# Workspace FFN: an eighth of the output bias added by VectorE as it moves the projected values from PSUM, in place of a bf16 product and ScalarE's copies

## The chip, the cores and the metric

The kernel runs on one core of a Trainium2 chip. Five engines work side by side and meet at semaphores: TensorE (PE; its weight loads are PEld), VectorE (DVE), ScalarE (ACT), GpSimd (POOL) and SyncE (SP), which starts most transfers. The metric is the time of one execution on the device, in microseconds (us), as the median of several runs.

## The reference

The program is a small decoder over x of shape 64 x 128 x 512: an attention, a feed-forward layer with ternary weights, a causal attention, and last the part that matters here, a workspace layer, run twice over the same weights:

```python
for _ in range(NB):                                   # NB = 2
    logits = _rms(x, norm_pre_w) @ compete_w.T + compete_b
    vals, idx = top_k(swapaxes(logits, 1, 2), 4)      # 4 tokens for each of 16 slots
    wgt = softmax(vals)
    written = einsum('bsk,bskd->bsd', wgt, (x @ write_w.T + write_b)[idx])
    ws = _rms(ws + written, norm_post_w)
    q, kk, vv = x @ wq.T + bq, ws @ wk.T + bk, ws @ wv.T + bv    # 8 heads of 64
    att = softmax(einsum('blhd,bshd->bhls', q, kk) * scale)      # over 16 slots
    x_b = einsum('bhls,bshd->blhd', att, vv) @ out_proj_w.T + out_proj_b
    x = _rms(x + x_b, norm_post_w)
```

The kernel uses that the slots are few: it projects the values with out_proj_w first, for each head and slot, which gives 8 x 16 = 128 rows of 512 for a batch (VO), and multiplies the 128 x 128 attention weights of a batch with them. For each token the weights of one head sum to 1, so those of its 8 heads sum to 8.

## The kernel before

The last stage, `workspace_ffn`, works on eight batches at a time, a unit. There are 16 units: 8 groups of eight batches, each passed through twice (`first` and `second` pass). Two neighbouring groups alternate, and the function `step(f, u, after)` of each engine interleaves the front half of unit f (transposes of X, logits, top four slots, new slots ws, keys and values) with the back half of unit f - 1, called u (scores, softmax, values, output). `units` runs 17 such steps: two written out, three turns of a loop of four, three written out. Steps 1 to 15 have both halves, step 16 only the back one. In half of them u is the second pass; its results are added to the first input by GpSimd (`add_first`) and stored.

No scheduler decides: each engine executes its own step in the order in which it is written, and waits at semaphores. The back half has, for each batch b of its eight:

- `value_out(b)` on TensorE, four products into the one bank `vo_ps`; it waits until the bank has been moved for the batch before (`vo_done`);
- `values(b)`, the move of `vo_ps` to `VO[b % 2]` (line 1918, on ScalarE before the change);
- `mix(b)` on TensorE into `xb_ps[b % 2]`: a product of 96 rows of ones with `out_b_parts` (line 1772), then the attention weights with VO (line 1773). `out_b_parts` holds the bias as the sum of three bf16 numbers, in rows 0, 32 and 64;
- `residual(b)` on VectorE, y = xb_ps + X (line 1619), its squares' sum on ScalarE (line 1925), 1/rms on GpSimd (lines 1493, 1495), and `final(b)` on VectorE (line 1630).

A f32 product of 512 columns is two instructions in the trace. From the front half of the same step the argument touches the chain of the top slots on VectorE, `lg` (line 1664) to `is_top` (1673), `w_raw` (1675) and `w_top` (1679), which TensorE turns at line 1839; the new slots `ws` (1718), turned at line 1879 and copied as `wsT` for the key and value products (1780); and `turn_att` (1764) with its copy `d_attT` (1930) on ScalarE, for which the first mix of a step waits. A tile's name has the prefix `d_` in the trace.

Of the kernel before, what the change touches and what calls it, by code (L numbers as in the profile page):

```python
# [12 lines left out]
BF16 = mybir.dt.bfloat16  # L13
# [896 lines left out]
class WorkspaceState:  # L910
# [3 lines left out]
    def __init__(self, nc, st, x, ident, workspace, compete_wT, compete_b, write_wT, write_b, wq, wkT, wvT, in_proj_cols,  # L914
# [14 lines left out]
        self.out_b_parts, self.ones_rows = sb("out_b_parts", [96, C], BF16), sb("ones_rows", [96, 128], BF16)  # L929
# [13 lines left out]
        self.out_b_row, self.out_b_part = self.y[:, 0, :], self.junk2[0:96, :]  # L943
# [11 lines left out]
        for dst, src in ((self.write_b_row[:, :], write_b), (self.out_b_row, out_b), (self.post_row[:, :], norm_post)):  # L955
            self.small.append((dst, src.rearrange("(o n) -> o n", o=1).to_broadcast([128, C])))
# [3 lines left out]
                        (self.WT[:, :, :], 0.0), (self.out_b_parts[:, :], 0.0), (self.ones_rows[:, :], 1.0),  # L960
# [3 lines left out]
def causal_attention(nc, x, ctx, ctxT, ident, after, causal_cols, x_out, w):  # L964
# [12 lines left out]
    with ExitStack() as st:  # L977
# [143 lines left out]
        def _(dve):  # L1121
# [7 lines left out]
            def step(t):  # L1129
# [45 lines left out]
                if t.k == 57:  # L1175
                    dve.wait_ge(w.small_in, 16 * 23)
                    dve.wait_ge(w.preset, 9)
# [3 lines left out]
                if t.k == 58:  # L1181
                    dve.tensor_copy(w.out_b_part, w.out_b_row[0:96, :]).then_inc(w.const_ready, 1)
                    dve.wait_ge(w.const_ready, 4)
                    dve.tensor_copy(w.out_b_parts[0:1, :], w.out_b_part[0:1, :]).then_inc(w.const_ready, 1)
                    dve.tensor_tensor(w.out_b_row[0:96, :], w.out_b_row[0:96, :], w.out_b_part, ALU.subtract).then_inc(w.const_ready, 1)
                if t.k == 59:
                    dve.wait_ge(w.const_ready, 6)
                    dve.tensor_copy(w.out_b_part, w.out_b_row[0:96, :]).then_inc(w.const_ready, 1)
                    dve.wait_ge(w.const_ready, 7)
                    dve.tensor_copy(w.out_b_parts[32:33, :], w.out_b_part[32:33, :]).then_inc(w.const_ready, 1)  # L1190
                    dve.tensor_tensor(w.out_b_row[0:96, :], w.out_b_row[0:96, :], w.out_b_part, ALU.subtract).then_inc(w.const_ready, 1)
                    dve.wait_ge(w.const_ready, 9)
                    dve.tensor_copy(w.out_b_parts[64:65, :], w.out_b_row[64:65, :]).then_inc(w.const_ready, 1)
# [151 lines left out]
def workspace_ffn(nc, x, w, x_out):  # L1345
# [13 lines left out]
    with ExitStack() as st:  # L1359
# [10 lines left out]
        write_b_row, post_row, out_b_parts, ones_rows, neg_half = w.write_b_row, w.post_row, w.out_b_parts, w.ones_rows, w.neg_half  # L1370
# [11 lines left out]
        is_top, e_top, w_raw, w_top = sb("is_top", [128, 128]), sb("e_top", [128, 128]), sb("w_raw", [128, 128]), sb("w_top", [128, 128])  # L1382
# [187 lines left out]
        def _(dve):  # L1570
# [16 lines left out]
            def step(f, u, after):  # L1587
# [25 lines left out]

                def residual(b):
# [45 lines left out]
                if f.exists():  # L1660
# [12 lines left out]
                    link(5, dve.tensor_tensor(is_top[:, :], lg_out[:, 0:128], lg[:, 0:128], ALU.not_equal))  # L1673
                    dve.wait_ge(e_top_done, n + 1)
                    dve.scalar_tensor_tensor(w_raw[:, :], e_top[:, :], 1.0, is_top[:, :], ALU.mult, ALU.mult, accum_out=w_sum[:, :]).then_inc(top_chain, 1)
# [3 lines left out]
                    dve.tensor_scalar(w_top[:, :], w_raw[:, :], w_inv[:, :], None, ALU.mult).then_inc(w_top_done, 1)  # L1679
# [17 lines left out]
                if u.exists():  # L1697
                    final(2)
# [10 lines left out]
                if u.exists():  # L1709
# [372 lines left out]
```

## Time and profile before

| | |
|---|---|
| median of 3 runs | 3844.27 us (3840.09 to 3847.71) |
| profiled execution, its time | 3834.83 us |
| its span in the trace | 3832.5 us |
| busy in the span: TensorE, its weight loads | 3597.9 us (94%), 1956.2 us (51%) |
| VectorE, ScalarE, GpSimd | 2818.8 us (74%), 2526.4 us (66%), 1747.7 us (46%) |
| `workspace_ffn`, from about 2930 us on | 902.5 us |

Times in rows are us from the start of the span unless marked ns. A row of a timeline gives start, length, engine, line of the kernel, operation, output <- inputs, shapes and a count; in brackets stands how long the engine had been idle before it, and which instruction ended that. Ends of matmuls are modelled, and the next one may start before the end shown. The profiled execution is one run, 9.4 us below the median of the others.

### The profile page before, as it was taken

What the parts mean: (1) busy time and instruction counts of PE and PEld (TensorE: products, weight loads), DVE (VectorE), ACT (ScalarE), POOL (GpSimd) and SP (SyncE); (2) the same over time, 40 slices, a digit from 0 to 9 for tenths busy, and PEclk for the clock granted to TensorE, in tenths of its full rate; (3) what the DMA queues carried; (4) which work ended last, traced back from release to release, by engine and by line L of the source; (5) the groups of instructions that cost most, each with busy time, mean ns of one, the idle gap of its engine ahead of it and who ended that gap; (6) DMA issues with size and microseconds to landing.
All of it is one profiled execution on the core that took longest, in us unless ns stands there. A gap on an engine that the chain in (4) does not pass through costs nothing. (4 is left out here: it accounts for less than half of the span.)

```text
span 3832.5 us, 87056 instructions
## 1 busy us (share of the span) xinstructions
PE 3597.9 (94%) x24963; PEld 1956.2 (51%) x24963; DVE 2818.8 (74%) x4439; ACT 2526.4 (66%) x6353; POOL 1747.7 (46%) x2154
## 2 busy tenths in 40 slices
PE   5999999999999999699999979999998999999997
PEld 1222222222222222277777857777776666556664
DVE  5888888888888889577777757777775555464645
ACT  2777777777777777577767757777774554545454
POOL 6444444444444443266666625454553233342524
PEclk9999999999999999899999999999998999999999
DMA  7777777777777777333333323333452022120302
GB/s 117 122 123 122 121 121 121 124 121 122 125 124 123 121 121 147 107 111 109 112 103 112 106 67 102 101 107 99 140 160 75 1 68 67 47 87 8 127 1 78
DMA packets 344164, 389.94 MB, mean 102 GB/s; under 512 B 58640, under 2 KB 223120, under 8 KB 343952
## 3 DMA queue, kind: packets, MB, share of 16 engines
q1 hardware_dynamic: 317328, 352.82, 42.3%
q10 hardware_dynamic: 26624, 34.63, 3.5%
q8 instruction: 93, 1.52, 0.2%
q14 instruction: 119, 0.97, 0.1%
HBM read 200.65 MB, written 84.93 MB: 75 GB/s over the span
## 5 line engine op out<-in xcount | busy, mean ns | idle before, releaser
L372 DVE TENSOR_REDUCE a_neg_max<-a_max_ps 128x2 f32<-128x1024 f32 x1024 | 1200.2, 1219 | 188.6 <-PE a_max_ps L461 165.3
L493 ACT ACTIVATE a_P<-a_ring_ps 128x512 f32<-128x512 f32 x2048 | 1084.5, 604 | 384.4 <-PE a_ring_ps L443 379.8
L461 PE MATMUL a_max_ps<-a_K,a_Q 96*128 96x512 bf16 x2048 | 621.2, 385 | 44.7 <-DMA a_K<-a_k_split 39.5
L443 PE MATMUL a_ring_ps<-a_Q,a_K 98*128 98x512 bf16 x2048 | 618.1, 382 | 5.5 <-DMA a_Q<-a_max_rows 3.3
L478 PE MATMUL a_pv_ps<-a_P,a_V 128*32 128x512 f32 x4096 | 544.9, 604 | 1.8 <-ACT a_out_sb L498 1.8
L443 PEld LDWEIGHTS a_ring_ps<-a_Q,a_K 98*128 98x128 bf16 x2048 | 158.1, 96 | 658.7 <-ACT a_P L493 585.2
L1295 ACT ACTIVATE c_P<-c_s_ps,c_bias 128x128 f32<-128x128 f32 x1024 | 363.3, 377 | 50.9 <-DVE c_bias L1140 44.1
L319 POOL TENSOR_SCALAR a_var_eps<-a_mean_var 128x1 f32<-128x1 f32 x64 | 12.2, 190 | 648.6 <-DVE a_mean_var L388 648.3
L461 PEld LDWEIGHTS a_max_ps<-a_K,a_Q 96*128 96x128 bf16 x2048 | 182.6, 98 | 224.3 <-DVE a_neg_max L372 46.6
L1135 DVE TENSOR_REDUCE c_neg_max<-c_s_ps 128x4 f32<-128x512 f32 x256 | 176.7, 690 | 128.8 <-PE c_s_ps L1230 128.0
L1266 PE MATMUL c_bank_b<-c_V,c_PT 128*128 128x32 f32 x2048 | 251.6, 267 | 2.9 <-DVE c_PT L1158 2.9
L1266 PEld LDWEIGHTS c_bank_b<-c_V,c_PT 128*128 128x128 f32 x2048 | 249.7, 192 | 5.3 <-DVE c_PT L1158 4.1
L1295 ACT ACTIVATION_READ_ACCUMULATOR c_P<-c_s_ps,c_bias 128x1 f32 x1024 | 221.4, 216 | 0.0
L478 PEld LDWEIGHTS a_pv_ps<-a_P,a_V 128*32 128x32 f32 x4096 | 81.1, 108 | 218.1 <-issue 214.2
L1228 PE MATMUL c_s_ps<-c_KD,c_qT 64*128 64x256 f32 x1024 | 181.7, 432 | 2.9 <-ACT c_P L1295 2.1
L1619 DVE TENSOR_TENSOR d_y<-d_xb_ps,d_X 128x512 f32<-128x512 f32 x128 | 88.2, 690 | 94.3 <-PE d_xb_ps L1773 91.4
L843 PE MATMUL b_t_ps<-w_had,b_u 128*128 128x256 f32 x512 | 155.9, 386 | 1.5 <-DVE b_u L763 1.5
L1240 PE MATMUL c_pT_ps<-c_identf,c_P 128*128 128x128 f32 x1024 | 156.8, 276 | 0.0
L844 PE MATMUL b_t_ps<-w_had,b_u 128*128 128x256 f32 x512 | 152.3, 379 | 0.0
L674 POOL TENSOR_TENSOR b_scaled<-b_o_in,b_r_in 128x512 f32<-128x512 f32 x64 | 82.7, 1292 | 150.6 <-DMA b_r_in<-recips 98.4
L1925 ACT ACTIVATE d_junk<-d_y 128x512 bf16<-128x512 f32 x128 | 80.3, 627 | 94.1 <-DVE d_y L1619 93.2
L1098 POOL TENSOR_SCALAR c_z<-c_x_in,c_mean_var,c_rstd 128x512 f32<-128x512 f32 x64 | 133.2, 2081 | 16.8 <-POOL c_rstd L1095 15.0
(259 smaller groups left out, 7100.5 us busy)
## 6 DMA issues: line engine op xcount, KB each, us to landing
a_Q<-a_q_split SPq DMA_DIRECT2D x384, 128.0 KB, 4.6
a_K<-a_k_split SPq DMA_DIRECT2D x384, 128.0 KB, 7.4
heads_out<-a_out_sb ACTq DMA_DIRECT2D x128, 256.0 KB, 4.1
a_x_in<-in_x_dram SPq DMA_DIRECT2D x64, 256.0 KB, 3.7
a_c_in<-in_ctx_dram SPq DMA_DIRECT2D x64, 256.0 KB, 4.1
a_cT_in<-in_ctxT_dram SPq DMA_DIRECT2D x64, 256.0 KB, 4.1
b_x_in<-in_x_dram SPq DMA_DIRECT2D x64, 256.0 KB, 2.8
b_o_in<-heads_out SPq DMA_DIRECT2D x64, 256.0 KB
```

The costliest lines, as they stand in the source:

```text
L372: dve.tensor_reduce(neg_max[:, p, 2 * u:2 * u + 2], max_ps[u % 2][:, :, :], AX.X, ALU.max, negate=True).then_inc(max_taken, 1)
L443: pe.matmul(ring(s, use_of(k))[:, :], K[i][:, h, n:n + 128], Q[i][:, h, :], start=True, stop=True).then_inc(scores_filled, 1)
L461: last = pe.matmul(max_ps[u % 2][:, j, :], Q[i][0:KROW, h, m:m + 128], K[i][0:KROW, h, :], start=True, stop=True)
L478: last = pe.matmul(pv_ps[32 * j:32 * j + 32, :], V[i][:, t, p * G + j, :], P[p][j][:, t, :], start=(t == 0), stop=(t == NT - 1))
L493: act.activation(P[p][k // NT][:, k % NT, :], ring(s, use_of(k))[:, :], ACT.Exp, scale=SCALE).then_inc(exp_done, 1)
L843: pe.matmul(t2_ps[:, k * 128:(k + 2) * 128], u[i][:, k, :], had[:, 0:256], start=True, stop=False)
L844: last = pe.matmul(t2_ps[:, k * 128:(k + 2) * 128], u[i][:, k + 1, :], had[:, 128:384], start=False, stop=True)
L1135: dve.tensor_reduce(neg_max[:, i, c * G:(c + 1) * G].rearrange("p (r g) -> p r g", r=2), s_ps[:, c % 2, :, 0:256].rearrange("p r (g k) -> ...
L1228: pe.matmul(s_ps[:, c % 2, r, 0:256], qT[i][rows, c, :], KD[i][rows, c], start=True, stop=False)
L1240: last = pe.transpose(pT_ps[c % 2][:, g, :], P[:, i, c * G + g, :], identf[:, :])
L1266: last = pe.matmul(bank_b[:, h * D:(h + 1) * D], PT[i][:, h, :], V[t.slot(back, 4)][:, h * D:(h + 1) * D], start=True, stop=True)
L1295: act.activation(P[:, i, h, :], s_ps[:, c % 2, g // 2, g % 2 * 128:g % 2 * 128 + 128], ACT.Exp, scale=SCALE, bias=bias[:, i, h:h + 1], acc ...
```

## The change

The bias no longer goes through TensorE. An eighth of it is added to each row of VO; since the weights of a token sum to 8 over the heads and slots, the product of mix(b) contains the whole bias. The add is made by VectorE in the move from PSUM, which ScalarE's copy did before. The eight moves of a step are placed by hand into VectorE's program. Seven operations of the stage before, which split the bias into three bf16 rows, make way for one that divides it by 8:

```diff
-        self.out_b_parts, self.ones_rows = sb("out_b_parts", [96, C], BF16), sb("ones_rows", [96, 128], BF16)
+        self.out_b_row = sb("out_b_row", [128, C])
...
                 if t.k == 58:
-                    dve.tensor_copy(w.out_b_part, w.out_b_row[0:96, :]).then_inc(w.const_ready, 1)
...
-                    dve.tensor_copy(w.out_b_parts[64:65, :], w.out_b_row[64:65, :]).then_inc(w.const_ready, 1)
+                    dve.tensor_scalar(w.out_b_row[:, :], w.out_b_row[:, :], 1.0 / 8, None, ALU.mult).then_inc(w.const_ready, 1)
...
+                def values(b):
+                    m = u.n() * NB + b
+                    dve.wait_ge(vo_filled, m + 1)
+                    at_least(dve, xb_filled, m - 1)
+                    dve.tensor_tensor(VO[b % 2][:, :], vo_ps[:, :], out_b_row[:, :], ALU.add).then_inc(vo_done, 1)
...
                     softmax_sum(0)
                     softmax_sum(1)
+                if u.exists():
+                    values(0)
+                    values(1)
...
                     link(5, dve.tensor_tensor(is_top[:, :], lg_out[:, 0:128], lg[:, 0:128], ALU.not_equal))
+                if u.exists():
+                    values(2)
+                if f.exists():
                     dve.wait_ge(e_top_done, n + 1)
...
                     residual(1)
+                    values(3)
...
                     residual(2)
+                    values(4)
                     final(1)
...
+                    values(5)
                     final(2)
...
+                    values(6)
                     final(4)
                     residual(5)
+                    values(7)
...
-                    pe.matmul(xb_ps[b % 2][:, :], ones_rows[:, :], out_b_parts[:, :], start=True, stop=False)
-                    pe.matmul(xb_ps[b % 2][:, :], attT[b // 4][:, b % 4, :], VO[b % 2][:, :], start=False, stop=True).then_inc(xb_filled, 1)
+                    pe.matmul(xb_ps[b % 2][:, :], attT[b // 4][:, b % 4, :], VO[b % 2][:, :], start=True, stop=True).then_inc(xb_filled, 1)
...
-                    act.activation(VO[b % 2][:, :], vo_ps[:, :], ACT.Copy).then_inc(vo_done, 1)
```

Two tiles are saved besides: w_raw is written over e_top and w_top over is_top. The line numbers after the change differ.

On VectorE, in the loop's fourth body (a step whose u is a first pass), between the mask of the top slots and the copy of the turned weights, the rows of before are these (REGISTER_ALU and ISA rows set a wait's count or a semaphore):

```order
L1673 TENSOR_TENSOR d_is_top<-d_lg_out,d_lg 128x128
L1590 REGISTER_ALU
L1675 SCALAR_TENSOR_TENSOR d_w_raw,d_w_sum<-d_e_top,d_is_top 128x128
L1676 REGISTER_ALU
L1677 RECIPROCAL d_w_inv<-d_w_sum 128x1
L1678 ISA
L1679 TENSOR_SCALAR d_w_top<-d_w_raw,d_w_inv 128x128
L1617 REGISTER_ALU
L1619 TENSOR_TENSOR d_y<-d_xb_ps,d_X 128x512
L1684 COPY d_WT<-d_F 128x8x16
L1630 SCALAR_TENSOR_TENSOR d_X<-d_y,d_y_r,d_post_row 128x512
```

and after the change these:

```order
L1672 TENSOR_TENSOR d_is_top<-d_lg_out,d_lg 128x128
L1579 REGISTER_ALU
L1606 REGISTER_ALU
L1608 TENSOR_TENSOR d_VO<-d_vo_ps,d_out_b_row 128x512
L1677 SCALAR_TENSOR_TENSOR d_e_top,d_w_sum<-d_e_top,d_is_top 128x128
L1678 REGISTER_ALU
L1679 RECIPROCAL d_w_inv<-d_w_sum 128x1
L1680 ISA
L1681 TENSOR_SCALAR d_is_top<-d_e_top,d_w_inv 128x128
L1615 TENSOR_TENSOR d_y<-d_xb_ps,d_X 128x512
L1606 REGISTER_ALU
L1608 TENSOR_TENSOR d_VO<-d_vo_ps,d_out_b_row 128x512
```

The move of batch 2 has come between is_top and the weights' chain (w_raw is now d_e_top, w_top is d_is_top), and that of batch 3 behind the residual of batch 1.

Also on VectorE, in the same body, from ws_sum to ws, before:

```order
L1708 TENSOR_TENSOR d_ws_sum<-d_F,d_ws_first 128x512
L1630 SCALAR_TENSOR_TENSOR d_X<-d_y,d_y_r,d_post_row 128x512
L1617 REGISTER_ALU
L1619 TENSOR_TENSOR d_y<-d_xb_ps,d_X 128x512
L1718 SCALAR_TENSOR_TENSOR d_ws<-d_ws_sum,d_ws_r,d_post_row 128x512
```

and after:

```order
L1713 TENSOR_TENSOR d_ws_sum<-d_F,d_ws_first 128x512
L1606 REGISTER_ALU
L1608 TENSOR_TENSOR d_VO<-d_vo_ps,d_out_b_row 128x512
L1626 SCALAR_TENSOR_TENSOR d_X<-d_y,d_y_r,d_post_row 128x512
L1615 TENSOR_TENSOR d_y<-d_xb_ps,d_X 128x512
L1606 REGISTER_ALU
L1608 TENSOR_TENSOR d_VO<-d_vo_ps,d_out_b_row 128x512
L1725 SCALAR_TENSOR_TENSOR d_ws<-d_ws_sum,d_ws_r,d_post_row 128x512
```

The moves of batches 6 and 7 now stand ahead of ws, the first before final(4), the second behind residual(5).

On TensorE, in the same body, from the transpose of lr to mix(2), before:

```order
L1829 MATMUL d_F<-d_identf,d_lr 128x128
L1764 MATMUL d_SC<-d_identf,d_att 128x128 x4
L1756 MATMUL d_vo_ps<-d_wo_sb,d_vd 32x512 x4
L1772 MATMUL d_xb_ps<-d_out_b_parts,d_ones_rows 128x512
L1773 MATMUL d_xb_ps<-d_VO,d_attT 128x512
L1756 MATMUL d_vo_ps<-d_wo_sb,d_vd 32x512 x4
L1772 MATMUL d_xb_ps<-d_out_b_parts,d_ones_rows 128x512
L1773 MATMUL d_xb_ps<-d_VO,d_attT 128x512
```

and after:

```order
L1835 MATMUL d_F<-d_identf,d_lr 128x128
L1771 MATMUL d_SC<-d_identf,d_att 128x128 x4
L1763 MATMUL d_vo_ps<-d_wo_sb,d_vd 32x512 x4
L1779 MATMUL d_xb_ps<-d_VO,d_attT 128x512
L1763 MATMUL d_vo_ps<-d_wo_sb,d_vd 32x512 x4
L1779 MATMUL d_xb_ps<-d_VO,d_attT 128x512
```

Only the bias product of each mix is gone; the order of all else is kept.

## Rows read from the trace of the kernel before

**Rows 1.** Table of stretches, the last: busy us of each engine (instructions), PEclk, DMA.
```profile
2930.00:3832.50 902.50, 822.49 (x6547) 535.50 (x6545) 470.27 (x911) 436.41 (x977) 317.23 (x460) 0.98 0.17 53
```

**Rows 2.** What TensorE waited for, 2930 to 3832.5: us, times, longest us.
```profile
PE d_F L1879 <- DVE d_ws L1718: 11.6, 7, 3.4
```

**Rows 3.** All instances of a line: minimum, median, maximum ns; first and last start.
```profile
L1772 PE MATMUL d_xb_ps<-d_out_b_parts,d_ones_rows x128: 376/389/587, 2999.0 to 3818.6; 96*128 96x512 bf16 x128
...
L1918 ACT ACTIVATE d_VO<-d_vo_ps x128: 575/597/662, 2994.8 to 3815.9; 128x512 f32<-128x512 f32 x128
...
L1619 DVE TENSOR_TENSOR d_y<-d_xb_ps,d_X x128: 675/692/693, 3000.2 to 3822.1; 128x512 f32<-128x512 f32 x128
...
L1630 DVE SCALAR_TENSOR_TENSOR d_out_sb<-d_y,d_y_r,d_post_row x64: 741/752/1860, 3110.0 to 3825.3; 128x512 f32<-128x512 f32 x64
```

**Rows 4.** Timeline of TensorE in one step: start us, us, what, count, idle before.
```profile
3426.99 1.04 PE L1756 MATMUL d_vo_ps<-d_wo_sb,d_vd 128*32 128x512 f32 x8
...
3429.70 0.39 PE L1772 MATMUL d_xb_ps<-d_out_b_parts,d_ones_rows 96*128 96x512 bf16 x1 [0.87 <-ACT d_attT L1930]
...
3429.93 1.02 PE L1773 MATMUL d_xb_ps<-d_VO,d_attT 128*128 128x512 f32 x2
...
3432.65 1.02 PE L1773 MATMUL d_xb_ps<-d_VO,d_attT 128*128 128x512 f32 x2
...
3433.60 1.07 PE L1756 MATMUL d_vo_ps<-d_wo_sb,d_vd 128*32 128x512 f32 x8
...
3435.69 0.27 PE L1839 MATMUL d_F<-d_identf,d_w_top 128*128 128x128 f32 x1
...
3448.45 1.07 PE L1756 MATMUL d_vo_ps<-d_wo_sb,d_vd 128*32 128x512 f32 x8
...
3450.53 0.60 PE L1879 MATMUL d_F<-d_identf,d_ws 128*128 128x128 f32 x4
...
3452.05 3.73 PE L1780 MATMUL d_F<-d_wsT,d_wk_sb 128*128 128x128 f32 x32
```

**Rows 5.** Timeline of VectorE in the same step.
```profile
3426.45 0.35 DVE L1612 RECIPROCAL d_sc_inv<-d_sc_sum 128x32 f32<-128x32 f32 x1
...
3431.08 0.69 DVE L1619 TENSOR_TENSOR d_y<-d_xb_ps,d_X 128x512 f32<-128x512 f32 x1 [2.28 <-PE d_xb_ps L1773]
...
3431.69 0.34 DVE L1664 TENSOR_SCALAR d_lg<-d_F,d_cb_col 128x128 f32<-128x128 f32 x1
...
3433.65 0.29 DVE L1673 TENSOR_TENSOR d_is_top<-d_lg_out,d_lg 128x128 f32<-128x128 f32 x1
...
3433.97 0.29 DVE L1675 SCALAR_TENSOR_TENSOR d_w_raw<-d_e_top,d_is_top 128x128 f32<-128x128 f32 x1
...
3434.71 0.68 DVE L1619 TENSOR_TENSOR d_y<-d_xb_ps,d_X 128x512 f32<-128x512 f32 x1
...
3449.16 0.74 DVE L1718 SCALAR_TENSOR_TENSOR d_ws<-d_ws_sum,d_ws_r,d_post_row 128x512 f32<-128x512 f32 x1
```

**Rows 6.** Timeline of ScalarE in the same step: V(2) of before.
```profile
3432.91 0.59 ACT L1918 ACTIVATE d_VO<-d_vo_ps 128x512 f32<-128x512 f32 x1
```

**Rows 7.** Timelines of VectorE and TensorE one step earlier, at ws.
```profile
3396.86 0.75 DVE L1718 SCALAR_TENSOR_TENSOR d_ws<-d_ws_sum,d_ws_r,d_post_row 128x512 f32<-128x512 f32 x1 [1.78 <-POOL d_ws_r L1495]
...
3397.76 0.63 PE L1879 MATMUL d_F<-d_identf,d_ws 128*128 128x128 f32 x4 [1.35 <-DVE d_ws L1718]
```

**Rows 8.** Timelines of TensorE and VectorE in the last step.
```profile
3795.87 1.06 PE L1756 MATMUL d_vo_ps<-d_wo_sb,d_vd 128*32 128x512 f32 x8 [2.38 <-ACT d_VO L1918]
...
3796.23 0.35 DVE L1612 RECIPROCAL d_sc_inv<-d_sc_sum 128x32 f32<-128x32 f32 x1
```

**Rows 9.** TensorE's timeline at a turn of the loop and one step without it; PEclk there.
```profile
3249.96 9.04 PE L1791 MATMUL d_SC<-d_A,d_XT 128*128 128x128 f32 x64 [2.68 <-issue]
...
3412.76 7.41 PE L1791 MATMUL d_SC<-d_A,d_XT 128*128 128x128 f32 x64
...
3252.00:3254.00 2.00, 2.00 (x12) 2.00 (x10) 0.00 (x0) 1.91 (x7) 0.00 (x0) 0.50 0.00 0
```

More of the change, by code:

```diff
@@ L954, in __init__ @@
             self.small.append((self.ws_in[i * S:(i + 1) * S, :], workspace))
-        for dst, src in ((self.write_b_row[:, :], write_b), (self.out_b_row, out_b), (self.post_row[:, :], norm_post)):
+        for dst, src in ((self.write_b_row[:, :], write_b), (self.out_b_row[:, :], out_b), (self.post_row[:, :], norm_post)):
             self.small.append((dst, src.rearrange("(o n) -> o n", o=1).to_broadcast([128, C])))
@@ L1381, in workspace_ffn @@
         top, neg_top = sb("top", [128, 8]), sb("neg_top", [128, 1])
-        is_top, e_top, w_raw, w_top = sb("is_top", [128, 128]), sb("e_top", [128, 128]), sb("w_raw", [128, 128]), sb("w_top", [128, 128])
+        is_top, e_top = sb("is_top", [128, 128]), sb("e_top", [128, 128])
         w_sum, w_inv = sb("w_sum", [128, 1]), sb("w_inv", [128, 1])
@@ L1673, in step @@
                     link(5, dve.tensor_tensor(is_top[:, :], lg_out[:, 0:128], lg[:, 0:128], ALU.not_equal))
+                if u.exists():
+                    values(2)
+                if f.exists():
                     dve.wait_ge(e_top_done, n + 1)
-                    dve.scalar_tensor_tensor(w_raw[:, :], e_top[:, :], 1.0, is_top[:, :], ALU.mult, ALU.mult, accum_out=w_sum[:, :]).then_inc(top_chain, 1)
+                    dve.scalar_tensor_tensor(e_top[:, :], e_top[:, :], 1.0, is_top[:, :], ALU.mult, ALU.mult, accum_out=w_sum[:, :]).then_inc(top_chain, 1)
                     dve.wait_ge(top_chain, n * LINKS + 6)
@@ L1678, in step @@
                     dve.wait_ge(w_top_done, n * 2 + 1)
-                    dve.tensor_scalar(w_top[:, :], w_raw[:, :], w_inv[:, :], None, ALU.mult).then_inc(w_top_done, 1)
+                    dve.tensor_scalar(is_top[:, :], e_top[:, :], w_inv[:, :], None, ALU.mult).then_inc(w_top_done, 1)
                 if u.exists():
                     residual(1)
+                    values(3)
                 if f.exists():
@@ L1746, in _ @@
         def _(pe):
-            pe.wait_ge(const_ready, 10)
+            pe.wait_ge(const_ready, 4)
             def step(f, u, after):
@@ L1838, in step @@
                     pe.wait_ge(w_top_done, n * 2 + 2)
-                    pe.transpose(ft[:, 0:128], w_top[:, :], identf[:, :]).then_inc(wT_filled, 1)
+                    pe.transpose(ft[:, 0:128], is_top[:, :], identf[:, :]).then_inc(wT_filled, 1)
                 if u.exists():
@@ L1913, in step @@
             def step(f, u, after):
-                def values(b):
-                    m = u.n() * NB + b
-                    act.wait_ge(vo_filled, m + 1)
-                    at_least(act, xb_filled, m - 1)
-                    act.activation(VO[b % 2][:, :], vo_ps[:, :], ACT.Copy).then_inc(vo_done, 1)
                 def squares(b):
@@ L1956, in step @@
                         act.activation(sc_exp[:, half, :], sc[:, half, :], ACT.Exp, scale=SCALE).then_inc(sc_exp_done, 1)
-                if u.exists():
-                    values(0)
                 if f.exists():
@@ L1963, in step @@
                 if u.exists():
-                    values(1)
                     copy_att(0)
@@ L1967, in step @@
                     copy_att(1)
-                    values(2)
                 if f.exists():
@@ L1973, in step @@
                 if u.exists():
-                    values(3)
                     squares(1)
-                    values(4)
                 if f.exists():
@@ L1984, in step @@
                     squares(3)
-                    values(5)
                     squares(4)
@@ L1994, in step @@
                 if u.exists():
-                    values(6)
-                    values(7)
                     squares(5)
```

17 lines of the change are left out of this document (3 added, 14 removed).

## The prediction

> **What bounds the kernel now.** I read the table of stretches first, then what TensorE waits for in the last stretch, then one step there engine by engine. The last stretch, from 2930 on, is the workspace FFN, the only part whose work changes. There TensorE is busy 822 of 902.5 us, VectorE 470, ScalarE 436 [rows 1]. So TensorE sets the pace, and neither of the two engines between which work moves is full. That is an average, though. TensorE's own waits there are few and name their places: 11.6 us in seven steps before the transposes of the new slots [rows 2], and in a step 0.87 us before the first bias product, for ScalarE's copy of the turned weights [rows 4]. A step is a chain on TensorE with short detours over ScalarE or VectorE, and the question is whether a detour gets longer.
>
> I take the step that starts near 3412. Names: vo(b) is value_out(b), V(b) the move of its PSUM bank to SBUF (values), mix(b) the attention product, R(b) residual, F(b) final. vo(b+1) needs V(b), because there is one bank vo_ps.
>
> **What goes.** 128 bf16 products [rows 3]. A row's length, 0.39 us, is not what one costs: the f32 product behind it starts 0.23 us later (3429.70, 3429.93 [rows 4]). Eight a step are 1.8 us, over 16 steps 29 us: the most that can be won. ScalarE loses 128 copies of 0.60 us, VectorE gains 128 adds. The nearest row for such an add is R, one operand in PSUM, one in SBUF, the same shape: 0.69 us, between 0.675 and 0.693 in 128 cases [rows 3]; the next operation on VectorE starts 0.61 us after it (3431.08, 3431.69 [rows 5]). So each move takes 0.09 us more for those who wait, and VectorE's sum, 128 x 0.61 = 78 us, fits its idle time of 432 us. The few constant operations that go ran in the stage before, on a VectorE with idle time, beside TensorE's work: I cost them at nothing (two to three operations of 0.4 to 0.9 us in a step, should that cover be missing).
>
> **What the order makes of it.** VectorE executes in program order, so V(b) starts only when what stands ahead of it is done.
>
> *V(0)* stands behind both softmax sums. The last reciprocal starts at 3426.45 and takes 0.35; with the 0.32 us by which one short operation follows another (3433.65, 3433.97), V(0) runs 3426.77 to 3427.46. A consumer on TensorE starts 0.10 us after a copy ends (3432.91 + 0.59, then vo(3) at 3433.60 [rows 4, 6]), so vo(1) starts at 3427.56 instead of 3426.99: +0.57. The turned weights and their copy follow vo(1), and mix(0) waited already for that copy (0.87 us), so the delay goes through. Its bias product is gone, but the f32 product must now show its own weight load, which hid behind it: I take 0.10 us for that (bounds 0 and 0.2, a bias product's start being all that the row shows). Product of mix(0): +0.57 - 0.23 + 0.10 = **+0.44**. mix(1) leaves out another 0.23: +0.21.
>
> *V(2)* is the large one. It stands behind is_top, at the end of the chain of the top four slots. That chain begins with lg behind R(0), which waits for mix(0): lg 3431.69 + 0.44 = 3432.13. is_top follows 1.96 us later (3431.69, 3433.65), V(2) 0.32 behind it, at 3434.41, done at 3435.10; vo(3) at 3435.20 instead of 3433.60: **+1.60**. Before, ScalarE did this copy at 3432.91, beside the chain. vo(3) followed the product of mix(1) by 0.95 us, so TensorE is ready for it at 3432.86 + 0.95 = 3433.81, and a stall of about 1.4 us opens. Queued behind V(2) are w_raw to w_top and R(1). w_raw starts 0.61 behind V(2), at 3435.02, and R(1) 0.74 behind w_raw (3433.97, 3434.71), at 3435.76, w_top being done by about then. The transpose of w_top, L1839, is itself 1.37 us late, at 3437.06, so it waits for nobody.
>
> *mix(2) to mix(6)* leave out 5 x 0.23 = 1.15 us. Their moves V(3) to V(5) come in time: V(3) runs 3436.37 to 3437.06, and vo(4) stands behind L1839; the longer products L1848 and L1868 cover the next. vo(7) needs V(6), which starts when vo(6) ends and is done about 0.05 us later than TensorE is free for it. At mix(6) the step is +0.45.
>
> *V(7)* now stands ahead of ws (L1718). vo(7) is late by 1.60 - 4 x 0.23 = 0.68, starts at 3449.13 and ends 1.07 us later; V(7) starts some 0.06 behind that (an estimate: R starts 0.13 us behind the end of its product, 3429.93 + 1.02, then 3431.08), 3450.26, ws 0.61 later, 3450.87, and ends at 3451.61 (before it started at 3449.16 [rows 5]). With 0.15 us to TensorE (3396.86 + 0.75, then 3397.76 [rows 7]) the transposes L1879 start at 3451.76 instead of 3450.53: **+1.23**, a stall of 1.23 - 0.45 = 0.78 us that this step did not have. mix(7) gives 0.23 back, and L1780, 1.52 us behind L1879 before, needs the copy wsT, which ended just in time; that takes about 0.13 more. End of the step: **+1.13 us**. The half whose F goes to X has eight such steps: 9.0 us.
>
> The other half, whose output gets the first input added on GpSimd, waited for ws anyway: VectorE 1.78 us for GpSimd's d_ws_r, TensorE 1.35 us for ws [rows 7]. Removed bias products win nothing there, nor does V(7) cost: GpSimd's chain decides. It starts from R(2)'s squares, behind the copies of g on ScalarE, behind the products behind vo(4). So it comes as late as vo(4): +1.60 - 0.23 = +1.37. Seven such steps: 9.6 us.
>
> The last step, without a next unit, has vo(1) at 3795.87 for V(0), which ScalarE ended just before; VectorE's reciprocal runs until 3796.58 [rows 8], so V(0) ends near 3797.2: +1.4 us. Its later adds may or may not fit between the F's (0 to 6 x 0.61 = 3.7 us more); I take 0, as its bias products go too.
>
> **Sum.** 9.0 + 9.6 + 1.4 = 20.0 us slower, of which the removed products have been subtracted. The profiled execution took 3834.83 us, which lies 9.4 under the median of the runs, 3844.27; so a profiled one would take 3854.8, and the median **3864 us**. The likeliest case alone has a range of 3854 to 3875: weight loads shown fully or not (0.1 us x 15), a V to TensorE at 0.15 in place of 0.10 (three times a step, 2.3 us), the last step's 3.7, steps in which the top chain runs at another pace.
>
> **Rivals.**
> A, *the bias products are won.* Then the moves would be hidden and 29 us go: 3815. For it speaks VectorE's idle half of the stretch. Against it, its idle time isn't at V(0), V(2) and V(7). It decides if V(2) ends before 3433.7, 1.4 us earlier than I have it. Chance 0.09.
> B, *only V(2) stalls.* If the stall at V(0) and that at ws were hidden, each step would lose 0.44 + 0.78 less, 15 x 1.2 = 18 us: 3846, no change. The wait of 0.87 us for the turned weights would have to be slack and not a chain. Chance 0.10.
> C, *the clock falls.* At the loop's turn TensorE stood 2.68 us and then ran 64 products in 9.04 us where they take 7.41, its granted clock 0.50 of full, that is 1.2 GHz, for two of these [rows 9]. Three stalls in ten microseconds (0.6, 0.9 and 1.4 us) may do the same: 15 x 1.6 = 24 us more, 3888. Against it: in the other half stalls of 0.9 and 1.35 us passed without. [...] Chance 0.12.
> D, *F behind V meets GpSimd.* In the half with the first input added, F takes 1.86 us in place of 0.75 when it runs into a GpSimd add [rows 3]. Now that V(5) and V(6) stand before it, F(2) or F(4) may start inside such an add: one in each of seven steps, 7.7 us, 3872. The Trainium skill ("SBUF — State Buffer", two separate sides) has the pair of ports that both use locked by whoever starts first, and V, with one SBUF operand, outside of it; R's even 0.69 us agrees. Chance 0.05.
> My forecast has 0.64.
>
> **Numbers.** Slower in my case, C and D, and a little of B: 0.82. A change of 0.2%, 7.7 us, is about what a measurement of this kernel can tell from none; within it: 0.09, most of B. Faster: 0.09, A. The range leaves out A and the upper part of C: 3848 to 3884.
>
> **What would show it.** The profile after should have: no bf16 product, vo(3) waiting for d_VO by 1.3 to 1.6 us in 15 steps, with is_top to d_VO 0.32 us on VectorE; ws transposes waiting in all steps of both halves; V at 0.69 us; ScalarE's busy time down 76 us, VectorE's up 88; no half clock inside a step. Wrong would be the forecast if vo(3) waits for nothing, or if the time of TensorE between vo(0) and L1780 shrinks.

## The result, and the profile after

The changed kernel takes 3848.9 us (median of 20 runs, 3844.6 to 3857.9), the kernel before beside it 3838.2 (20 runs, 3832.3 to 3847.7): 1.0028 times as long, 95% interval 1.0021 to 1.0034, or 10.7 us slower. The forecast was 20.0 us slower, from 3844.3 to 3864. The three runs shown before the change lay 6.1 us above what 20 runs give; that shifts the forecast's time, not its difference. The profiled execution of after took 3844.60 us, its span is 3842.5, 10.0 above that of before.

The workspace stage of after, first its table of stretches (busy us and instructions of PE, PEld, DVE, ACT, POOL; PEclk, DMA), then what TensorE waited for:

```profile
2930.00:3842.50 912.50, 808.70 (x6400) 515.62 (x6400) 545.71 (x1032) 366.61 (x848) 317.46 (x458) 0.98 0.16 52
```

```profile
PE d_vo_ps L1763 <- DVE d_VO L1608: 25.8, 29, 3.7
PE d_F L1885 <- DVE d_ws L1725: 17.6, 16, 3.4
PE d_xb_ps L1779 <- ACT d_attT L1930: 11.5, 13, 1.0
...
PE d_F L1809 <- PEq L54: 6.9, 1, 6.9
```

VectorE's busy time is up 75.4 us, ScalarE's down 69.8, TensorE's down 13.8 [rows 1], and TensorE has a wait that it hadn't, for VectorE's V (25.8 us), and waits for ws in 16 steps where it was 7 [rows 2]. The same step as in [rows 4, 5], TensorE and then VectorE; it starts 0.54 us later than in before (scores at 3413.30, before 3412.76):

```profile
3427.93 1.06 PE L1763 MATMUL d_vo_ps<-d_wo_sb,d_vd 128*32 128x512 f32 x8 [0.23 <-DVE d_VO L1608]
...
3430.67 1.12 PE L1779 MATMUL d_xb_ps<-d_VO,d_attT 128*128 128x512 f32 x2 [0.87 <-ACT d_attT L1930]
3431.63 0.27 PE L1835 MATMUL d_F<-d_identf,d_lr 128*128 128x128 f32 x1
...
3435.63 1.06 PE L1763 MATMUL d_vo_ps<-d_wo_sb,d_vd 128*32 128x512 f32 x8 [1.25 <-DVE d_VO L1608]
3436.63 1.12 PE L1779 MATMUL d_xb_ps<-d_VO,d_attT 128*128 128x512 f32 x2
3437.59 0.27 PE L1845 MATMUL d_F<-d_identf,d_is_top 128*128 128x128 f32 x1
3437.80 1.06 PE L1763 MATMUL d_vo_ps<-d_wo_sb,d_vd 128*32 128x512 f32 x8
...
3449.97 1.07 PE L1763 MATMUL d_vo_ps<-d_wo_sb,d_vd 128*32 128x512 f32 x8
...
3452.60 0.63 PE L1885 MATMUL d_F<-d_identf,d_ws 128*128 128x128 f32 x4 [0.51 <-DVE d_ws L1725]
...
3453.93 3.83 PE L1786 MATMUL d_F<-d_wsT,d_wk_sb 128*128 128x128 f32 x32
```

```profile
3431.83 0.69 DVE L1615 TENSOR_TENSOR d_y<-d_xb_ps,d_X 128x512 f32<-128x512 f32 x1 [1.87 <-PE d_xb_ps L1779]
3432.44 0.34 DVE L1663 TENSOR_SCALAR d_lg<-d_F,d_cb_col 128x128 f32<-128x128 f32 x1
...
3434.40 0.29 DVE L1672 TENSOR_TENSOR d_is_top<-d_lg_out,d_lg 128x128 f32<-128x128 f32 x1
3434.89 0.69 DVE L1608 TENSOR_TENSOR d_VO<-d_vo_ps,d_out_b_row 128x512 f32<-128x512 f32 x1 [0.20 <-DVE d_is_top L1672]
```

That is the forecast's picture: vo(3) waits 1.25 us for V(2), which stands behind is_top. It does so in twelve of the 15 steps; in the other three (the first and the last two) the wait is 0.62 us. A length on the axis of the whole execution tells the rest. The columns below are worked out from each profile: **set-up**, from VectorE's first constant operation (d_cw, in causal attention) to TensorE's first X transposes of the workspace stage; **steps**, from the first score product of the first step that has them to that of the last, 15 steps; **end**, from there to the end of the span.

```
kernel                set-up   15 steps   end
before                102.0     803.1     47.4
after                  97.0     823.0     46.8
```

So the steps lost 20.0 us, and 5.0 us came back before they began, in a place that the prediction had costed at nothing. (Another 2.9 us of this pair of profiles lie ahead of the constants, in stages with the same code, 1.4 between the X transposes and the first step's score products, 0.7 at the end. The last two go with TensorE's clock: before is at half clock for 14.8 us between these transposes and the score products, after for 9.6; in the end before has a piece of 6.8 us at 3797 where after has one of 3.4.)

### The profile page after: what moved, and what is told of

Read it like the earlier page. It is cut to its first block and busy times, and to the rows that moved or that the text cites. A ratio compares the mean times of both kernels' runs of the same rounds, so it can differ in the third digit from the quotient of the medians.

```text
span 3842.5 us, 86727 instructions
## 1 busy us (share of the span) xinstructions
PE 3586.1 (93%) x24773; PEld 1941.2 (51%) x24835; DVE 2891.0 (75%) x4561; ACT 2458.4 (64%) x6225; POOL 1750.3 (46%) x2152
## 5 line engine op out<-in xcount | busy, mean ns | idle before, releaser
L1763 PE MATMUL d_vo_ps<-d_wo_sb,d_vd 128*32 128x512 f32 x1024 | 137.2, 608 | 26.2 <-DVE d_VO L1608 25.8
L1779 PE MATMUL d_xb_ps<-d_VO,d_attT 128*128 128x512 f32 x256 | 142.4, 638 | 14.8 <-ACT d_attT L1930 11.5
```

## The experiments

Each kernel was run 6 to 20 times beside before on the same chip; differences in us below are its ratio to that before, times 3838. An interval of 0.0010 is 3.8 us. All columns:

```
kernel                median us  ratio (95% interval)     diff   set-up  15 steps  end
after                 3848.9     1.0028 (1.0021, 1.0034)  +10.7   97.0    823.0    46.8
no_setup              3829.6     0.9975 (0.9966, 0.9985)   -9.6   97.0    805.1    44.7
no_product            3823.1     0.9953 (0.9938, 0.9968)  -18.0   97.0    795.0    44.4
vector_and_product    3855.1     1.0036 (1.0022, 1.0051)  +13.8   97.0    829.2    48.3
v2_early              3852.7     1.0032 (1.0020, 1.0043)  +12.3   97.0    823.8    49.5
scalar_234            3836.1     0.9990 (0.9981, 0.9999)   -3.8   97.0    806.6    50.1
scalar_67             3846.7     1.0019 (1.0010, 1.0028)   +7.3   97.0    817.8    49.2
setup_moved           3831.4     0.9978 (0.9969, 0.9986)   -8.4   97.0    803.4    47.4
setup_spread          3838.6     0.9986 (0.9977, 0.9995)   -5.4   99.2    803.3    47.5
before_again          3839.9     0.9997 (0.9986, 1.0007)   -1.2  102.2    805.1    44.5
before_third          3836.9     1.0001 (0.9991, 1.0010)   +0.4  101.9    803.3    47.4
pool_bias             3831.9     0.9982 (0.9973, 0.9991)   -6.9   97.0    806.5    47.1
pool_bias2            3850.7     1.0020 (1.0011, 1.0030)   +7.7   97.0    822.7    44.4
pool_bias3            3823.9     0.9968 (0.9958, 0.9978)  -12.3   97.0    797.0    45.7
```

**no_setup: before without the set-up.**

```diff
-                if t.k == 58:
-                    dve.tensor_copy(w.out_b_part, w.out_b_row[0:96, :]).then_inc(w.const_ready, 1)
...
-                    dve.tensor_copy(w.out_b_parts[64:65, :], w.out_b_row[64:65, :]).then_inc(w.const_ready, 1)
...
-            pe.wait_ge(const_ready, 10)
+            pe.wait_ge(const_ready, 3)
```

> The kernel before without the seven VectorE operations that split the output bias into three bf16 parts (the parts stay zero, so the bias is left out of the output; the bf16 product and ScalarE's copies stay). Between the first constant operation and the first X transposes of the workspace stage the profile of after is 5.0 us shorter than that of before: two seven-operation pieces hold VectorE in causal attention, TensorE then waits 1.17 us at 2863.85, and the granted clock is 0.50 to 0.65 from 2864 to 2872, which it is not after the change. Theory S (the set-up costs what that stretch shows): 4 to 6 us less than before, about 3833, and no stretch at half clock near there. Rival N (the earlier stages only differed from one execution to the next): within 1.5 us of before, 3838, the dip in the clock elsewhere or still there.

9.6 us less: Theory S, with more than it asked for. (The seven operations stand in two pieces, of three and of four.) Before shows how few microseconds of set-up cost 5. VectorE at the second piece, then TensorE behind it, then PEclk (the column behind the POOL pair):

```profile
2858.72 0.39 DVE L1188 CAST d_junk<-d_y 96x512 bf16<-96x512 f32 x1
2859.14 0.28 DVE L1190 COPY d_out_b_parts<-d_junk 1x512 bf16<-1x512 bf16 x1
2859.46 0.69 DVE L1191 TENSOR_TENSOR d_y<-d_y,d_junk 96x512 f32<-96x512 f32 x1
2860.18 0.88 DVE L1193 CAST d_out_b_parts<-d_y 1x512 bf16<-1x512 f32 x1
2861.09 0.69 DVE L1135 TENSOR_REDUCE c_neg_max<-c_s_ps 128x4 f32<-128x512 f32 x1
```

```profile
2862.08 0.60 PE L1240 MATMUL c_pT_ps<-c_identf,c_P 128*128 128x128 f32 x4
2863.85 1.08 PE L1266 MATMUL c_bank_b<-c_V,c_PT 128*128 128x32 f32 x8 [1.17 <-DVE c_PT L1158]
...
2869.59 1.23 PE L1228 MATMUL c_s_ps<-c_KD,c_qT 64*128 64x256 f32 x4
...
2872.91 0.70 PE L1228 MATMUL c_s_ps<-c_KD,c_qT 64*128 64x256 f32 x4
```

```profile
2864.00:2868.00 4.00, 4.00 (x24) 3.31 (x24) 3.77 (x6) 1.65 (x9) 1.59 (x2) 0.65 0.44 170
2868.00:2872.00 4.00, 4.00 (x18) 2.96 (x18) 0.61 (x1) 1.99 (x9) 0.00 (x0) 0.50 0.00 0
2872.00:2876.00 4.00, 4.00 (x29) 2.87 (x28) 3.76 (x13) 2.70 (x13) 2.42 (x3) 1.00 0.57 162
```

Four operations in a row hold the next c_PT back, TensorE waits 1.17 us, and then runs at 1.2 GHz (PEclk 0.50) for 6.8 us (0.35 and 0.50 of full missing in 4 us each) until 2872: the same four products take 1.23 us at 2869.59 and 0.70 at 2872.91. The whole stretch, before and then no_setup:

```profile
2837.00:2939.00 102.00, 92.18 (x673) 70.73 (x673) 82.55 (x168) 63.10 (x296) 48.76 (x47) 0.94 0.38 122
```

```profile
2836.45:2933.44 96.99, 88.65 (x673) 68.28 (x672) 77.04 (x161) 63.17 (x295) 48.18 (x47) 0.97 0.41 129
```

The same 673 products keep TensorE busy 3.5 us longer in before: that is the half clock. Its waits for c_PT are 1.5 us longer (2.9 for 1.4). Together 5.0. VectorE itself is idle 20 of the 97 us of no_setup, so its idle time is real, but not where the piece stands: in the same round it is idle for 0.37 and 0.40 us there, against a piece of 2.3 (no_setup):

```profile
2857.88 0.69 DVE L1135 TENSOR_REDUCE c_neg_max<-c_s_ps 128x4 f32<-128x512 f32 x1 [0.37 <-PE c_s_ps L1217]
...
2860.98 0.69 DVE L1135 TENSOR_REDUCE c_neg_max<-c_s_ps 128x4 f32<-128x512 f32 x1 [0.40 <-PE c_s_ps L1217]
```

**setup_moved and setup_spread: the same seven operations elsewhere.** The first puts them at the start of VectorE's first step of the workspace stage (TensorE waits for them at its first mix only), the second leaves one at the end of each of seven steps of causal attention:

```diff
# setup_moved
+                if f.exists() and isinstance(f.q, int) and f.n() == 0:
+                    row, part = y[0:96, 0, :], junk2[0:96, :]
+                    dve.tensor_copy(part, row).then_inc(const_ready, 1)
...
# setup_spread, and so on to t.k == 64
+                if t.k == 58:
+                    dve.wait_ge(w.const_ready, 3)
+                    dve.tensor_copy(w.out_b_part, w.out_b_row[0:96, :]).then_inc(w.const_ready, 1)
```

> The kernel before with its seven set-up operations moved out of causal attention, to the start of VectorE's first step of the workspace stage, where VectorE stands idle for most of 30 us; TensorE waits for them at the first mix only. Theory S: the stretch from the first constant operation to the first X transposes becomes 97.0 us long, as in every kernel without them there (102.0 before), and the whole gain of the run without the set-up stays: 3829 to 3832 beside 3839. Rival F (they cost as much where they now stand, since the first step waits for VectorE's chain): the stretch is 97.0, but the one from the first X transposes to the first score products grows by 4 or more, 3835 or more.

> The kernel before with its seven set-up operations spread: one at the end of each of seven steps of causal attention, in place of three and four together. VectorE does the same 3.4 us of work. Theory C (the price is TensorE's 1.17 us wait behind four operations in a row and the 8 us at half clock after it): no wait of 1 us there, no stretch at half clock, and 97.0 to 98.5 us from the first constant operation to the first X transposes; 8 us below before, 3831. Rival V (VectorE sets the pace of causal attention, so its work counts wherever it stands): 100 to 102 us, at most 4 below before.

Moved, they cost nothing that can be told: 8.4 us below before, where leaving them out gave 9.6, and the whole computation is done. Spread, the stretch is 99.2 us:

```profile
2839.67:2938.90 99.23, 88.69 (x673) 68.33 (x673) 79.93 (x168) 62.78 (x296) 48.46 (x47) 0.97 0.39 126
```

TensorE's products take 88.7 us as without the set-up, and no half clock stands behind the operations; it still waits for c_PT five times, 3.6 us, at most 0.8, and that is the 2.2 us. (All profiles have a piece of half clock at the end of the stretch, where TensorE stands 7 us before the X transposes.) So the same work costs 2.2 us of waits when it is spread, and 1.5 of waits and 3.5 of clock when it stands in two pieces. Both theories were half right.

**before_again, before_third: before, unchanged.**

> The kernel before, unchanged, profiled once more. The set-up's stretch shows 5.0 us, but the kernels without it measure 8.5 to 10 us below before. Theory P (the first profile was of a quick execution, 3834.8 beside a median of 3839): this one shows the same 102 us from the first constant operation to the first X transposes and 3 to 5 us more in the steps of the workspace stage, where single steps were 1.7 us apart. Rival D (the set-up's price varies, through the clock): the stretch is longer than 102 in this execution.

> The kernel before once more, for a profile. Both profiles of it so far were of executions at a granted clock of 0.987 on the mean, where most of its executions show 0.984 and are 4 to 6 us longer; those without the set-up in causal attention show 0.987 to 0.988. Theory C (an ordinary execution of before loses clock in a place that theirs does not): at 0.984 or 0.985 the profile shows 10 to 20 us more at half clock, and where. Rival R (scattered pieces of 3.4 us, as in every profile): more of them, in no one place.

The stretch is 102.2 and 101.9 long: the 5 us repeat. They do not make the 8.4 to 9.6 measured. Executions of before lie between 3829 and 3850 us, and go with their mean granted clock (3844 us on the mean at 0.983, 3838 at 0.985, 3836 at 0.986); those of no_setup and setup_moved show 0.986 to 0.988. In the three profiles the 6.8 us behind the set-up repeat, and single pieces of 3.4 us stand in other places each time (at 1947, at 1927, at 1843 and 2004), as Rival R has it. But all three were of quick executions (0.986, 0.987), so Theory C was not tried. Where an ordinary one loses the other 4 us stays open.

**no_product and vector_and_product: the two halves of the change, apart.** Both without the set-up. The first drops the bf16 product and keeps ScalarE's copies; the second keeps the product and has VectorE move:

```diff
# no_product
-                    pe.matmul(xb_ps[b % 2][:, :], ones_rows[:, :], out_b_parts[:, :], start=True, stop=False)
...
# vector_and_product
-                    act.activation(VO[b % 2][:, :], vo_ps[:, :], ACT.Copy).then_inc(vo_done, 1)
+                    dve.tensor_tensor(VO[b % 2][:, :], vo_ps[:, :], write_b_row[:, :], ALU.add).then_inc(vo_done, 1)
```

> The same without the bf16 product as well (bias left out of the output): ScalarE still moves the projected values. In the profile of after a mix takes 0.96 us from its start to the next instruction where product and bias product took 0.43 + 0.66 = 1.09, since the f32 product's weight load now shows for 0.10. Theory P (each removed product is worth 0.13 us on a TensorE that is the bound): 128 x 0.13 = 17 us below the run without the set-up, about 3817. Rival P23 (each is worth its whole 0.23 us): 29 us below, 3804. Rival H (TensorE waits for something else anyway, and the product was hidden): less than 8 us below, 3825 or more.

> VectorE moves the projected values at the places of the changed kernel, and the bf16 product stays in mix (over zero parts, no set-up operations; the moves add the write bias row as a stand-in, so the output is another one). Theory W (the moves cost by themselves what the prediction's stalls say, 1.33 us of net loss a step plus the 1.04 that the product's removal gives back, in 15 steps): 17 us above after, about 3866, and 33 above the run without the set-up. Rival C (the waits for VectorE take the product in: a product before a wait costs nothing): less than 8 us above after, 3850 to 3857.

With ScalarE's copies the product is worth 8.4 us (10.2 in the steps), 0.07 to 0.08 a product: between P and H. Of the 10.2, 9.1 are in the eight steps whose F goes to X, and 1.1 in the seven others, where the prediction had it win nothing. With VectorE's moves it is worth 3.1, less than the intervals of the two runs can tell from none (6.1 in the steps): TensorE would stand there anyway, Rival C. The moves cost 23.4 us with the product and 28.7 without (24.0 and 28.1 in the steps, 1.6 to 1.9 a step). So the result divides, by these runs' differences, into -9.6 (set-up) - 8.4 (product) + 28.7 (moves) = +10.7, each term good to some 6 us.

**v2_early: V(2) out of its place.**

```diff
                     dve.tensor_scalar(lg[:, 0:128], F[U_LG % 3][:, 0:128], cb_col[:, :], None, ALU.add).then_inc(lg_done, 1)
+                if u.exists():
+                    values(2)
...
                     link(5, dve.tensor_tensor(is_top[:, :], lg_out[:, 0:128], lg[:, 0:128], ALU.not_equal))
-                if u.exists():
-                    values(2)
```

> The changed kernel with one move put elsewhere: values(2) right behind the addition that makes lg, ahead of the top-k chain, in place of behind its end. The prediction puts 1.4 us of stall a step on that place (vo(3) waits 1.25 us for it in the profile of after, and the products behind it). Theory V2: the stall goes, but the chain ends 0.6 us later; the transpose behind mix(2) then comes up to 1 us early for it. 15 steps x 0.9 to 1.4 = 13 to 21 us below after, 3828 to 3836. Rival T (the top-k chain is the path: w_top is then waited for as long as V(2) was): 3845 to 3850.

Nothing gained: 823.8 in the steps, against 823.0, and 3852.7 us, so Theory V2 falls; Rival T's wait came only in part. Its TensorE in the same step, then its V(2):

```profile
3430.96 1.06 PE L1763 MATMUL d_vo_ps<-d_wo_sb,d_vd 128*32 128x512 f32 x8 [0.23 <-DVE d_VO L1608]
...
3437.35 1.07 PE L1763 MATMUL d_vo_ps<-d_wo_sb,d_vd 128*32 128x512 f32 x8
3438.34 1.12 PE L1779 MATMUL d_xb_ps<-d_VO,d_attT 128*128 128x512 f32 x2
3439.71 0.33 PE L1845 MATMUL d_F<-d_identf,d_is_top 128*128 128x128 f32 x1 [0.24 <-DVE d_is_top L1681]
3440.90 1.06 PE L1763 MATMUL d_vo_ps<-d_wo_sb,d_vd 128*32 128x512 f32 x8 [0.87 <-DVE d_VO L1608]
```

```profile
3436.43 0.69 DVE L1608 TENSOR_TENSOR d_VO<-d_vo_ps,d_out_b_row 128x512 f32<-128x512 f32 x1 [0.62 <-PE d_vo_ps L1763]
```

vo(3) waits no more, but the transpose of the weights does, 0.24, and vo(4), 0.87, for V(3). From vo(1) to vo(4) it is 9.94 us (3430.96, 3440.90); in after 9.87 (3427.93, 3437.80). From R(0) to V(3) VectorE has one nearly unbroken row of work (3431.83 to 3437.50 in after), which leaves V(3) little room to end sooner by another order. The place tried here was itself too early by 0.62 us, in which VectorE stood and waited for vo(2). A place inside the top chain, where vo(2) is just done, was not tried.

**scalar_234 and scalar_67: moves given back to ScalarE.**

```diff
# VectorE; and 2, 4 (scalar_234), or 6, 7 (scalar_67)
-                    values(3)
...
# ScalarE, at its old place
+                    values(3)
```

> The changed kernel with V(2), V(3) and V(4) moved by ScalarE again, as plain copies at their old places (the bias is left out of those three of eight blocks). Moving V(2) alone within VectorE's order gave nothing: TensorE's wait went from vo(3) (1.25 us) to vo(4) (0.87) and the transpose of the weights (0.24). Theory W (VectorE's work from R(0) to V(3) is the path there, whatever its order: two moves of 0.6 us fewer): 1.2 to 1.6 us a step less, 15 steps, 18 to 24 us below after, 3825 to 3831. Rival E (what VectorE gains there it loses at R(5) to ws, so the end of the step is where the time is set): less than 8 us below after, 3841 or more.

> The changed kernel with V(6) and V(7) moved by ScalarE again (the bias is left out of those two of eight blocks). The prediction puts 1.2 us of a first pass step there (ws and its transposes behind two moves) and 0.4 to 0.8 on the rest. Theory E (V(6) and V(7) are ahead of ws on VectorE, and TensorE waits for ws: 0.51 us in a first pass step, 1.59 in a second pass step): 0.6 us x 2 less a step where the wait is long, 15 steps x 0.7 to 1.2: 10 to 18 us below after, 3831 to 3839. Rival W (the middle of the step is what counts): less than 6 us below, 3843 or more.

```profile
PE d_F L1880 <- DVE d_ws L1720: 17.6, 16, 3.4
...
PE d_vo_ps L1758 <- DVE d_VO L1608: 10.5, 15, 3.7
```

```profile
PE d_vo_ps L1761 <- DVE d_VO L1608: 25.2, 28, 3.7
PE d_F L1883 <- DVE d_ws L1723: 12.1, 7, 3.4
```

scalar_234 (first fence) takes 16.5 us off the steps: Theory W, by less than it said. scalar_67 (second) has the waits for ws back at 7, and takes only 5.2 us off the steps and 3.4 off the time: Theory E falls. 4.4 of them are in the eight steps whose F goes to X. Of the 28.1 us that the moves cost in the steps, 16.5 come back with V(2) to V(4) and 5.2 with V(6) and V(7); if such parts add up, which no run shows, 6.4 are left for V(0), V(1) and V(5).

**pool_bias, 2 and 3: the bias on a third engine.** The three say that a version should have neither the product nor the moves nor the set-up. X is read by nobody but R between the products for g and the next step, so GpSimd can add the bias row to it in place, 8 additions a step:

```diff
+            def add_bias(u, bs):
+                for b in bs:
+                    pool.tensor_tensor(X[u.pair()][:, b, :], X[u.pair()][:, b, :], out_b_row[:, :], ALU.add).then_inc(biased, 1)
...
                 def residual(b):
                     dve.wait_ge(xb_filled, m + 1)
+                    dve.wait_ge(biased, m + 1)
```

> The whole computation, with neither the bf16 product nor VectorE's moves: ScalarE copies as before, the bias row is loaded to a tile of its own (no set-up operations), and GpSimd adds it to the X that the residual reads, in place, 8 additions of 128x512 a step, in its idle time ahead of the attention weights (it waits there 5.8 us in a first pass step of X and 15 us in the others; such an addition takes it 1.3 us). Theory G (GpSimd's idle time takes them): as the run without product and set-up, 3823, to 3830, so 10 to 16 us below before. Rival D (the additions delay att or the rstd chain, or slow VectorE's operations beside them): each step 1 us longer, 3838 or more.

> The version with the bias added by GpSimd, with its additions moved. In it five of the steps whose X is of a first pass took 1.6 to 2.3 us more than without the additions, the others 0.0: there three additions stood ahead of the chain that makes rstd. Now none does: five behind x_r, two behind att, one behind the first finish; in the other steps all eight stay at the start. Theory R (the rstd chain was what they delayed): those steps within 0.7 us of the run without additions, steps 796 to 800 in all, 3823 to 3827. Rival T (eight additions are too many for a first pass step's GpSimd, wherever they stand): 1.5 us or more a step stays, 3830 or more.

> GpSimd's additions a third time. Five additions behind x_r made the steps with a first pass X up to 5.4 us longer: beside them VectorE's normalisation of X (128x512, 0.54 us each by itself) takes up to 1.50 us, four in 5.73 us in place of 1.91, and the additions themselves 1.42 in place of 1.25. Now in those steps three additions stand ahead of the rstd chain (they ended as the moments came), none beside the normalisation, three behind att, one behind each of the first two finishes. Theory N (what cost the time was the normalisation beside the additions): normalisation at 0.54 us everywhere, steps 796 to 800 us, 3822 to 3827. Rival Q (GpSimd's queue: y_r comes later behind the additions in steps that also make the output): 1 us or more a step stays in those, 3829 or more.

The second, meant to be better, was 14.6 us slower than the first, and Theory R fell. The chain to rstd was not what the additions hurt. VectorE and GpSimd in it, then VectorE's normalisation in all of pool_bias3 (minimum, median, maximum ns):

```profile
3417.05 1.92 DVE L1639 TENSOR_SCALAR d_X<-d_X,d_moments,d_rstd 128x512 f32<-128x512 f32 x4 [2.36 <-POOL d_rstd L1501]
...
3421.05 5.73 DVE L1639 TENSOR_SCALAR d_X<-d_X,d_moments,d_rstd 128x512 f32<-128x512 f32 x4
```

```profile
3420.81 7.10 POOL L1486 TENSOR_TENSOR d_X<-d_X,d_out_b_row 128x512 f32<-128x512 f32 x5 [0.34 <-POOL d_x_r L1512]
```

```profile
L1635 DVE TENSOR_SCALAR d_X<-d_X,d_moments,d_rstd x56: 537/542/549, 2978.0 to 3630.2; 128x512 f32<-128x512 f32 x56
```

Four normalisations take 1.92 us alone and 5.73 beside GpSimd's additions, whose mean is 1.42 (7.10 / 5) where their median over the stage is 1.27. The normalised X goes to TensorE's transposes, and the clock falls behind their waits. TensorE and its clock in the same step of pool_bias2:

```profile
3422.69 0.65 PE L1805 MATMUL d_F<-d_identf,d_X 128*128 128x128 f32 x4 [0.49 <-DVE d_X L1639]
3424.10 0.65 PE L1805 MATMUL d_F<-d_identf,d_X 128*128 128x128 f32 x4 [0.76 <-ACT d_XT L1948]
3425.51 0.65 PE L1805 MATMUL d_F<-d_identf,d_X 128*128 128x128 f32 x4 [0.76 <-ACT d_XT L1948]
3426.91 1.07 PE L1805 MATMUL d_F<-d_identf,d_X 128*128 128x128 f32 x4 [0.76 <-ACT d_XT L1948]
```

```profile
3423.00:3427.00 4.00, 1.73 (x13) 1.03 (x11) 4.00 (x4) 2.17 (x4) 4.00 (x4) 1.00 0.00 0
3427.00:3430.40 3.40, 3.40 (x20) 1.38 (x24) 3.26 (x7) 1.63 (x3) 1.22 (x2) 0.50 0.00 0
```

In its 15 steps TensorE is at half clock for 34.1 us, in those of pool_bias3 for 6.8. The difference of 27.3 us at half is up to 13.7 us of work lost, about half of the 25.7 us between the two. With no addition beside them pool_bias3 takes 797.0 us in the steps, 2.0 more than the run without any bias, and 0.9968 times before (0.9958 to 0.9978): 12 us faster than before, 23 faster than the change, the whole computation done. Rival Q keeps a part: two of the steps whose output needs GpSimd for the first input too are 2.1 and 2.2 us longer than without the bias, of which up to 1.7 are a piece of half clock in each, where TensorE waits 2.6 us for ws.

## Why the prediction was half right

Direction and the steps held; the sum missed what happened outside them, and one cause was put at a place where a whole stretch is it. Same step, before to after, less the 0.54 us:

```
                        forecast   measured
vo(1)                    +0.57      +0.40
mix(0), f32 product      +0.44      +0.20
vo(3)                    +1.60      +1.49   (stall 1.4 / 1.25)
transpose of w_top       +1.37      +1.36
vo(7)                    +0.68      +0.98
transposes of ws         +1.23      +1.53   (stall 0.78 / 0.51)
K projection             +1.13      +1.34
```

- **The constant operations at nothing: the step that failed.** The prediction took VectorE's idle time in causal attention for cover and kept a bound for it only in brackets. The idle time is there (20 of 97 us) but not around the pieces, and the bound left out the clock. The pieces cost 5.0 us in the profile, 1.5 of waits and 3.5 of clock, and 8.4 to 9.6 in the runs, nearly the whole error of 9.3 us in the difference (20.0 for 10.7). The part of it that no profile shows, about 4 us, stays unexplained.
- **V(0)** was placed a little late, +0.40 for +0.57; the delay did pass through the wait of 0.87 us for the turned weights, which is unchanged.
- **V(2), the large one**: time and stall came near the forecast, in part by luck. R(0) and with it is_top came 0.23 us earlier than said (+0.21 for +0.44), and V(2) stood 0.49 us behind is_top, not 0.32; the two nearly cancel. The reason given, one place behind is_top, is too narrow: it is one place in a row of VectorE work that is too long. v2_early moved the stall and kept the time, scalar_234 took 16.5 us away.
- **mix(2) to mix(6)**: mis-sized. The 0.10 us for a shown weight load was put at mix(0) alone; the f32 product is 1.12 us long in place of 1.02 at each of these mixes, so each gives back 0.13, not 0.23. vo(3) to vo(7) shrank by 0.51 = 4 x 0.13, forecast 0.92. That is why vo(7) and ws came later than said.
- **V(7) ahead of ws**: a wait for ws in all 16 steps came as forecast. V(6) and V(7) together are worth 0.55 us in each of the eight steps whose F goes to X (scalar_67; forecast 0.78 for the stall) and 0.1 in the others, where the prediction had V(7) cost nothing.
- **Sum of the steps**: 18.6 forecast (9.0 and 9.6), 20.0 measured: 12.3 in the eight steps whose F goes to X, of which 1.7 are one piece of half clock that before happened not to have, and 7.7 in the seven others (0.7 to 1.3 each, forecast 1.37). Without that piece it is 10.6 and 7.7, so the near agreement of the sum (18.3 for 18.6) is luck in part: one half was put 1.6 too low, the other 1.9 too high.
- **The last step**: forecast +1.4, and the pair of profiles has -0.7. But before is at half clock for 6.8 us there, at 3797, and before_again, which is not, is 2.3 us shorter than after. The term is not settled.
- **Rivals.** A and B didn't come. C didn't: PEclk is 0.98 in the stage, as before; stalls of 0.2, 0.9 and 1.25 us inside 10 us passed at full clock. That was not safe to assume: in before a wait of 1.17 us in causal attention was followed by the half clock, and in pool_bias2 four waits of 0.5 to 0.8 us within 5 us were. D came in small: in six of the seven steps two F's meet a GpSimd add and take 1.07 to 1.38 us, where in before none of theirs is over 0.8; that is 0.95 us of VectorE's time a step. It doesn't show as a cost, those steps coming out below their forecast. (The F's near 1.86 us [rows 3] stand in the last two steps, in both kernels.)
- **The base**: the median of three runs stood 6.1 us too high, and the predicted time with it.

## What to carry to other kernels

Work in one-off set-up costs what its place costs: look at what waits right behind that place, not at the engine's idle share of the stage, and at TensorE's clock behind it, before calling it free. When a move between engines opens a stall, ask whether one instruction is misplaced or the engine's work between two points of the chain is too long; one kernel with the order changed and one with the work taken off help to tell them apart. To judge an edit with two halves, time each half alone: here a saving of 18 us (product and set-up) was spent on moves worth 29, and a third engine could have the work for about 6 (2.0 in the steps), once its additions stood clear of VectorE's normalisation.

## What the runs showed of the hardware

- One wait of 1.17 us of TensorE was followed by 6.8 us at 1.2 GHz in causal attention, in each of three profiles; waits of 0.2, 0.9 and 1.25 us within 10 us in the steps of after were not. In pool_bias2 three or four waits of 0.3 to 0.8 us within 5 us (0.49 and three of 0.76 in the step shown) went with 3.4 or 6.8 us at 1.2 GHz in five of the six steps that have them.
- VectorE's normalisation of a 128x512 f32 tile (tensor_scalar, both operands in SBUF) takes 0.54 us, and up to 1.50 beside a GpSimd addition; four took 5.73 for 1.92. The Trainium skill ("SBUF — State Buffer", Who interferes with whom) has tensor_scalar among the operations that can take the pair of ports that VectorE shares with GpSimd, whoever starts first keeping it; the trace agrees, with both engines' rows longer.
- The f32 product of a mix is 1.02 us long behind the bf16 product, and 1.12 when it stands right behind the products of vo; behind the transposes of ws it is 1.02 again. That the 0.10 us are its weight load is inferred.
- Executions of one kernel on one core spread over 5 to 21 us, and go with the mean granted clock: about 3 us for 0.001 in before.
